# A transformer decoder on one core: four PSUM banks in one ring, query parts added on VectorE, two scalings on ScalarE, one tile for the rests of gates and values

## What is computed

```python
for i in range(DEPTH):                       # 6 layers
    x = attn_layer(shift_tokens(x), ...) + x # 16 heads of 64, window 64, rotary, l2norm of q and k
    x = ffn_layer(shift_tokens(x), ...) + x  # layernorm, 256 -> 2 x 682, a * gelu(gate), 682 -> 256
```

## Time and profile before

| | us |
|---|---|
| median of three runs | 2921.83 |
| the profiled execution | 2921.92 |
| its span, first to last instruction | 2920.1 |
| PE busy | 2776.2 (95%) |
| PE weight loads busy | 2447.4 (84%) |
| DVE busy | 2311.1 (79%) |
| ACT busy | 1978.6 (68%) |
| POOL (GpSimd) busy | 1362.4 (47%) |

### The profile page before, as it was taken

How to read it: one execution, slowest core, us unless ns; L and a number is a source line. 1 busy time by engine, 2 the same in 40 slices (tenths; PEclk the granted TensorE clock), 3 DMA queues, 4 the chain that set the end, 5 groups by cost and what they waited for, 6 DMA issues and landing times. The chain is left out here.

```text
span 2920.1 us, 80983 instructions
## 1 busy us (share of the span) xinstructions
PE 2776.2 (95%) x26408; PEld 2447.4 (84%) x26408; DVE 2311.1 (79%) x7881; ACT 1978.6 (68%) x5719; POOL 1362.4 (47%) x1436
## 2 busy tenths in 40 slices
PE   8889999999999999999999999999999999999996
PEld 6668888888888888888888888888888888888885
DVE  5478888878888888888877888887888877887773
ACT  4367767767776776777667667766776776676663
POOL 4454444535444453544445454544444453545440
PEclk9999999999999999999999999999999999999997
DMA  5212132333213324221333222143213233110110
GB/s 163 73 37 82 63 107 76 133 98 109 82 63 107 114 82 138 83 82 63 122 102 127 81 91 82 63 141 128 83 64 106 76 133 99 54 31 23 38 26 21
DMA packets 140063, 251.67 MB, mean 86 GB/s; under 512 B 14718, under 2 KB 78728, under 8 KB 138632
## 3 DMA queue, kind: packets, MB, share of 16 engines
q1 hardware_dynamic: 139224, 249.36, 26.0%
q10 hardware_dynamic: 688, 0.39, 0.0%
HBM read 137.72 MB, written 80.55 MB: 75 GB/s over the span
## 5 line engine op out<-in xcount | busy, mean ns | idle before, releaser
L904 PE MATMUL project<-w_qkv,xT 128*128 128x512 f32 x3456 | 892.0, 402 | 16.6 <-DVE with_sin L1275 11.8
L904 PEld LDWEIGHTS project<-w_qkv,xT 128*128 128x128 f32 x3456 | 621.9, 188 | 154.9 <-issue 12.4
L1179 POOL TENSOR_SCALAR sums_sq<-sums_sq 128x8 f32<-128x8 f32 x384 | 92.2, 240 | 1243.8 <-DVE sums_sq L1270 1238.3
L1124 ACT ACTIVATE probs<-probs,shift 128x128 f32<-128x128 f32 x1536 | 595.2, 390 | 73.6 <-DVE shift L1343 73.2
L1343 DVE CUSTOM_DVE_ANT_0 probs<-score,mask,query_scale 128x128 f32<-128x128 f32 x1536 | 439.8, 347 | 161.4 <-PE score L996 150.6
L959 PE MATMUL wide<-nT,w_up 128*128 128x256 f32 x3456 | 478.9, 288 | 13.8 <-ACT gates L1105 3.6
L959 PEld LDWEIGHTS wide<-nT,w_up 128*128 128x128 f32 x3456 | 439.8, 191 | 44.7 <-ACT gates L1105 24.0
L1355 DVE TENSOR_SCALAR probs<-probs,sums 128x128 f32<-128x128 f32 x1536 | 426.6, 341 | 13.6
L1073 ACT ACTIVATE with_sin<-project 128x512 f32<-128x512 f32 x384 | 230.5, 600 | 188.8 <-PE project L904 188.5
L1188 POOL TENSOR_TENSOR sums_sq<-sums_sq,half 128x8 f32<-128x8 f32 x192 | 321.4, 1674 | 16.0
L1185 POOL TENSOR_TENSOR query_scale<-sums_sq,half 128x8 f32<-128x8 f32 x192 | 317.7, 1655 | 22.2 <-POOL sums_sq L1179 12.3
(11 more groups left out here) (119 smaller groups left out, 4656.4 us busy)
## 6 DMA issues: line engine op xcount, KB each, us to landing
w_parts_scratch<-staging SPq DMA_DIRECT2D x120, 519.0 KB, 3.0
staging<-in_w_next SPq DMA_DIRECT2D x60, 519.0 KB, 5.0
w_qkv<-w_parts_scratch SPq DMA_DIRECT2D x20, 1536.0 KB, 9.2
v_mid<-v SPq DMA_DIRECT2D x192, 128.0 KB, 2.3
w_up<-w_parts_scratch SPq DMA_DIRECT2D x20, 682.0 KB, 6.3
y_in<-y_scratch SPq DMA_DIRECT2D x48, 256.0 KB, 3.7
res<-y_scratch SPq DMA_DIRECT2D x48, 256.0 KB, 2.7
y_scratch<-res SPq DMA_DIRECT2D x40, 256.0 KB, 4.1
```

The source lines that it names most:

```text
L904: last = pe.matmul(project[(x - 1) % 2][:], xT[a][:, h, t * P:(t + 1) * P], w_qkv[w][:, h, c, g, :], start=(h == 0 and (a, w) == PASSES[0] ...
L1124: last = act.activation(probs[:, k, cols], probs[:, k, cols], ACT.Exp, bias=shift[:, k, i:i + 1], scale=-1.0, accum_out=sums[:, k, i:i + 1])
```

## The change

- **Ring.** `project`, `turned` and `wide` give way to `ring`, four banks taken in turn by all fills of `input`, `unit`, `turn`, `turned`, `norm_turn`, `gate` and `value`, in `PE_ORDER`; the last one, `turned 3 1`, takes the bank two further on. `bank_free` now waits for the readers of the fill that had the same bank before (`fill_before`). Semaphores are counted by kind of fill.
- **Query parts.** DVE adds `with_sin` into `with_cos` for a query (128x512), and PE transposes four pieces as for a key.
- **Scalings.** Of the eight scalings of two heads in a slot, `scale 0 1` and `scale 3 0` are done by ACT (four `Copy` activations with a scale), after an `inverse` on DVE.
- **Rests.** The 42 columns of the values and, from row 64, the 42 of the gates share one 128-column tile, made with `gate 2`; `value 2` has one tile. A new DVE item `rest` multiplies them. A layer's fetch of `w_up` has four more DMAs (42 columns each).
- **Orders.** All four lists are changed, and the item `exp_table` (a tiny Exp that loads the table ahead of `exp 3 0`) is gone. Slot 1 is written out.

```diff
+RING = 4
...
 PE_ORDER = [
-    ("scores", 0), ("mix", 3), ("unit", 1, 0), ("unit", 1, 1), ("project_out", 0), ("unit", 1, 2), ("unit", 1, 3),
-    ("turned", 0, 0), ("project_out", 1), ("turned", 0, 1), ("turn", 1, 0), ("turn", 1, 1),
-    ("scores", 1), ("mix", 0), ("turn", 1, 2), ("unit", 1, 4), ("unit", 1, 5), ("turn", 1, 3), ("turned", 1, 0), ("norm_turn",),
-    ("input",), ("turned", 1, 1),
-    ("scores", 2), ("mix", 1), ("unit", 0, 0), ("unit", 0, 1), ("gate", 0), ("turned", 2, 0), ("unit", 0, 2), ("gate", 1),
-    ("unit", 0, 3), ("turned", 2, 1), ("gate", 2),
-    ("scores", 3), ("mix", 2), ("value", 0), ("turn", 0, 0), ("unit", 0, 4), ("value", 1), ("down", 0), ("turn", 0, 1),
-    ("turn", 0, 2), ("value", 2), ("down", 1), ("turned", 3, 0), ("unit", 0, 5), ("turn", 0, 3), ("turned", 3, 1), ("down", 2),
+    ("scores", 0), ("mix", 3), ("unit", 1, 0), ("unit", 1, 1), ("unit", 1, 2), ("project_out", 0), ("unit", 1, 3),
+    ("project_out", 1), ("turned", 0, 0), ("turned", 0, 1), ("turn", 1, 1),
+    ("scores", 1), ("mix", 0), ("unit", 1, 5), ("unit", 1, 4), ("turn", 1, 0), ("turn", 1, 3), ("turned", 1, 0), ("turn", 1, 2),
+    ("input",), ("turned", 1, 1), ("norm_turn",),
+    ("scores", 2), ("mix", 1), ("unit", 0, 0), ("gate", 0), ("gate", 1), ("unit", 0, 1), ("gate", 2), ("value", 0),
+    ("unit", 0, 2), ("turned", 2, 0), ("unit", 0, 3), ("turned", 2, 1),
+    ("scores", 3), ("mix", 2), ("value", 1), ("down", 0), ("unit", 0, 5), ("value", 2), ("turn", 0, 2), ("turn", 0, 1),
+    ("down", 1), ("unit", 0, 4), ("turn", 0, 3), ("turned", 3, 0), ("turn", 0, 0), ("down", 2), ("turned", 3, 1),
 ]
 ACT_ORDER = [
-    ("out", 3), ("unit", 1, 0), ("unit", 1, 1), ("exp", 0, 0), ("exp", 0, 1), ("unit", 1, 2), ("unit", 1, 3), ("copied", 0, 0),
-    ("copied", 0, 1), ("split_high", 0, 0), ("turn", 1, 0), ("turn", 1, 1), ("split_high", 0, 1), ("exp", 1, 0), ("turn", 1, 2),
-    ("out", 0), ("unit", 1, 4), ("exp", 1, 1), ("unit", 1, 5), ("turn", 1, 3), ("copied", 1, 0), ("input",), ("copied", 1, 1),
-    ("norm_turn",), ("exp", 2, 0), ("unit", 0, 0), ("exp", 2, 1), ("unit", 0, 1), ("gate", 0), ("copied", 2, 0), ("out", 1),
-    ("unit", 0, 2), ("gate", 1), ("unit", 0, 3), ("copied", 2, 1), ("gate", 2), ("exp_table",), ("exp", 3, 0), ("value", 0),
-    ("split_high", 1, 0), ("turn", 0, 0), ("split_high", 1, 1), ("unit", 0, 4), ("out", 2), ("value", 1), ("exp", 3, 1),
-    ("turn", 0, 1), ("turn", 0, 2), ("value", 2), ("copied", 3, 0), ("unit", 0, 5), ("turn", 0, 3), ("copied", 3, 1),
+    ("out", 3), ("unit", 1, 0), ("unit", 1, 1), ("exp", 0, 0), ("exp", 0, 1), ("unit", 1, 2), ("scale", 0, 1),
+    ("split_high", 0, 0), ("split_high", 0, 1), ("unit", 1, 3), ("copied", 0, 0), ("copied", 0, 1), ("turn", 1, 1),
+    ("exp", 1, 0), ("exp", 1, 1), ("unit", 1, 5), ("unit", 1, 4), ("turn", 1, 0), ("turn", 1, 3), ("copied", 1, 0),
+    ("turn", 1, 2), ("out", 0), ("input",), ("copied", 1, 1), ("norm_turn",), ("exp", 2, 0), ("unit", 0, 0), ("exp", 2, 1),
+    ("gate", 0), ("unit", 0, 1), ("gate", 1), ("out", 1), ("gate", 2), ("split_high", 1, 0), ("unit", 0, 2), ("copied", 2, 0),
+    ("value", 0), ("copied", 2, 1), ("unit", 0, 3), ("split_high", 1, 1), ("out", 2), ("exp", 3, 0), ("value", 1),
+    ("unit", 0, 5), ("exp", 3, 1), ("scale", 3, 0), ("turn", 0, 2), ("value", 2), ("turn", 0, 1), ("unit", 0, 4),
+    ("copied", 3, 0), ("turn", 0, 3), ("turn", 0, 0), ("copied", 3, 1),
 ]
 DVE_ORDER = [
-    ("mask", 0, 0), ("mask", 0, 1), ("out", 3), ("rotate", 1, 0), ("rotate", 1, 1), ("scale", 0, 0), ("scale", 0, 1),
-    ("rotate", 1, 2), ("rotate", 1, 3), ("add_out",), ("mask", 1, 0), ("norm_stats",), ("mask", 1, 1), ("scale", 1, 0),
-    ("norm_apply",), ("scale", 1, 1), ("split_low", 0, 0), ("out", 0), ("input",), ("mask", 2, 0), ("mask", 2, 1),
-    ("norm_turn",), ("scale", 2, 0), ("rotate", 0, 0), ("split_low", 0, 1), ("rotate", 0, 1), ("scale", 2, 1), ("out", 1),
-    ("rotate", 0, 2), ("rotate", 0, 3), ("mask", 3, 0), ("value", 0), ("low", 0), ("value", 1), ("mask", 3, 1), ("low", 1),
-    ("scale", 3, 0), ("value", 2), ("scale", 3, 1), ("low", 2), ("out", 2), ("split_low", 1, 0), ("split_low", 1, 1),
-    ("residual",),
+    ("mask", 0, 0), ("mask", 0, 1), ("out", 3), ("rotate", 1, 0), ("rotate", 1, 1), ("scale", 0, 0), ("inverse", 0, 1),
+    ("rotate", 1, 2), ("add_out",), ("rotate", 1, 3), ("mask", 1, 0), ("mask", 1, 1), ("norm_stats",), ("scale", 1, 0),
+    ("scale", 1, 1), ("norm_apply",), ("split_low", 0, 0), ("split_low", 0, 1), ("out", 0), ("input",), ("mask", 2, 0),
+    ("norm_turn",), ("mask", 2, 1), ("rotate", 0, 0), ("scale", 2, 0), ("scale", 2, 1), ("rotate", 0, 1), ("rest",),
+    ("value", 0), ("out", 1), ("rotate", 0, 2), ("mask", 3, 0), ("low", 0), ("rotate", 0, 3), ("value", 1), ("mask", 3, 1),
+    ("low", 1), ("inverse", 3, 0), ("out", 2), ("value", 2), ("low", 2), ("scale", 3, 1), ("residual",), ("split_low", 1, 0),
+    ("split_low", 1, 1),
 ]
 POOL_ORDER = [
-    ("rotate", 1, 0), ("rotate", 1, 1), ("rotate", 1, 2), ("rotate", 1, 3), ("norm_stats",), ("rotate", 0, 0), ("rotate", 0, 1),
-    ("norm_turn",), ("rotate", 0, 2), ("rotate", 0, 3),
+    ("rotate", 1, 0), ("rotate", 1, 1), ("rotate", 1, 2), ("rotate", 1, 3), ("norm_stats",), ("norm_turn",), ("rotate", 0, 0),
+    ("rotate", 0, 1), ("rotate", 0, 2), ("rotate", 0, 3),
 ]
 SHIFT_WIDE = 112
+ODD_FILL = ("turned", 3, 1)
...
+RING_FILLS, RING_BANK = [], []
+_next = 0
 for _item in PE_ORDER:
...
+    if _item[0] in ("unit", "turn", "turned", "input", "norm_turn", "gate", "value"):
+        for _half in range(HALVES if _item[0] == "input" else 1):
+            RING_FILLS.append((_item, _half))
+            if _item == ODD_FILL:
+                RING_BANK.append((_next + RING // 2) % RING)
+            else:
+                RING_BANK.append(_next)
+                _next = (_next + 1) % RING
+assert _next == 0
...
+def fill_before(n, item, half=0):
+    at, slots = RING_FILLS.index((item, half)), 0
+    j = at
+    while slots > -3:
+        j -= 1
+        if j < 0:
+            j, slots = j + len(RING_FILLS), slots - 1
+        if RING_BANK[j] == RING_BANK[at] and (not isinstance(n, int) or is_filled(n + slots, RING_FILLS[j][0])):
+            return n + slots, RING_FILLS[j]
+    return None
...
+    slot(Slot(1, next_batch=2, ffn_batch=0, chunk=0))
     for layer in range(DEPTH):
-        with eng.Fori(1, BATCH - 1) as b:
+        with eng.Fori(1 if layer else 2, BATCH - 1) as b:
...
-                dst = self.up[part][:, :, FFN:2 * FFN] if blk == 3 else self.up[part][:, :, 0:FFN]
+                at, rest = (FULL, 2 * FULL + GATE_REST) if blk == 3 else (0, 2 * FULL)
                 cols = cols.rearrange("p (k n) -> p k n", k=HALVES)
+                sp.dma_start(self.up[part][:, :, rest:rest + FFN_REST].bitcast(FP32), cols[:, :, FULL:FFN]).then_inc(self.fetched[blk], 16)
+                dst, cols = self.up[part][:, :, at:at + FULL], cols[:, :, 0:FULL]
...
-        project = [ctx.enter_context(nc.psum_tensor(f"project{i}", [P, GROUP], FP32)) for i in range(2)]
+        ring = [ctx.enter_context(nc.psum_tensor(f"ring{i}", [P, GROUP], FP32)) for i in range(RING)]
         score = [ctx.enter_context(nc.psum_tensor(f"score{i}", [P, GROUP], FP32)) for i in range(2)]
-        turned = ctx.enter_context(nc.psum_tensor("turned", [P, GROUP], FP32))
         mix = ctx.enter_context(nc.psum_tensor("mix", [P, 2, TOKENS], FP32))
...
-        wide = ctx.enter_context(nc.psum_tensor("wide", [P, 2, TOKENS], FP32))
...
+                if kind == "unit":
+                    g, u = item[1:]
+                    m = n if g else n + 1
+                    if u < 4:
+                        pe.wait_ge(parts_ready, rotation(m, g, u))
+                    else:
+                        pe.wait_ge(unit_read[g], unit_fill(m, g, u))
+                elif kind == "turn":
+                    g, u = item[1:]
+                    pe.wait_ge(turn_read[g], turn_fill(n if g else n + 1, g, u))
+                elif kind == "input":
+                    pe.wait_ge(input_read, (n + 1) * HALVES + half + 1)
+                    pe.wait_ge(input_split, (n + 1) * HALVES + half + 1)
+                elif kind == "turned":
+                    k, j = item[1:]
+                    pe.wait_ge(probsT_copied, n * HEADS + QUAD_HEADS * k + 2 * j + 2)
+                elif kind == "norm_turn":
+                    pe.wait_ge(xn_read, f + 1)
+                elif kind == "gate" and item[1] == 2:
+                    pe.wait_ge(rest_read, f + 1)
+                elif kind == "gate":
+                    pe.wait_ge(gate_read, f * 3 + item[1] + 1)
+                else:
+                    pe.wait_ge(value_read, f * 3 + item[1] + 1)
...
+                    if u % 2:
+                        pe.wait_ge(rotated, rotation(m, g, u))
+                    else:
+                        pe.wait_ge(query_added, m * 4 + 2 * g + u // 2 + 1)
+                    bank_free(s, item)
```

(50 more changed lines are left out.)

233 lines of the change are left out of this document (111 added, 122 removed).

## The result

The changed kernel takes **2720.1 us** (median of 4 runs, 2718.1 to 2723.1) against 2921.5 in the same session: ratio 0.931, 95% interval 0.930 to 0.933. The direction and most of the mechanism held. What was off is the stall, the time in a slot in which PE waits: it was taken at 3.0 us a slot and measures 2.2.

The account below looks back on a forecast made before the run. PE was taken to fill the slot of 56.70 us, with about 4.0 of it stall. Span 2920.1 - 118 (PE's work) - 46 (stall) + 9 (later transfer) = 2765, with 1.8 around the span 2767 us; range 2722 to 2800, chance 0.61.

Parts of the forecast that it names:

- the stall: PE's waiting time in a slot: forecast to fall from 4.0 to 3.0 us, 46 us over 46 slots.
- the later transfer: Raw chunks asked for later, behind y's later store: ACT waits some 1.3 us in 30 slots; +9 us, bounds 0 and 39.
- The walk: Following each wait through the four new lists with measured pitches: a slot of 52.7 us, stall 2.5.
- a stall of 1.7 behind ACT's copies: Between scores 1 and scores 2, the ring hands PE each bank only after ACT's copy: 1.7 of 9.6 us.
- the margin for hand-overs: Added to the walk's stall of 2.5 for small hand-over times and late transfers, giving 3.0 and a slot of 53.2.
- The stall of before: About 4.0 us of the old slot, largest before scores 2, where PE was said to wait for DVE's scaling and norm.
- PE's work: Fewer transposes (1.74 us a slot) and value matmuls (0.71): 2.45 us a slot, 118 us in 48 slots, all on the path.
- DVE: Four adds +2.44 us, eight scaling instructions -1.58, rest 0: net +0.9 a slot, to 48.4.
- ACT: Eight activations 128x128 come in at 0.30 us each: +2.4 us, ACT at 43.1 a slot.
- Work only: Rival: the ring's new waits cost what the old ones did, so only PE's work is saved; 2813 us, chance 0.18.
- DVE keeping its idle: Rival "slower": in-order lists leave DVE's 9.1 us of idle, slot 57.5 us, time 2959 us; chance 0.05.
- The GpSimd rival: Every query add on DVE waits 0.9 us for GpSimd's power: 2890 us; clearest mechanism of "part lost", chance 0.08.

Follow-up runs that it names:

- l: The kernel before with one edit: scale 0 1 moved from DVE to ACT, behind unit 1 2; 2859 us, ratio 0.980.
- e: The changed kernel with a query's two parts added by PE again (eight transposes a turn) and DVE's four adds gone; 2754 us, ratio 0.943.
- f: The changed kernel with value 2 given two tiles again, six more matmuls 128x256; 2745 us, ratio 0.940.
- p: The changed kernel with the lists of before, except rest ahead of mask 3 0 and scale 0 1 on ACT; ring kept; 2915 us, ratio 0.999.
- j: The changed kernel with only scale 0 1 put back on DVE, scale 3 0 staying on ACT; 2766 us, ratio 0.947.
- m: The changed kernel with split_low 1 before residual, split_high 0 after unit 1 3's square, Exp table fetched ahead, add_out after rotate 1 3, norm_stats after scale 1 0; 2735 us.
- g: The changed kernel with split_low 1 0 and 1 1 ahead of residual in DVE's list; 2719 us, ratio 0.931.
- h: The changed kernel with split_high 0 0 and 0 1 behind the square of unit 1 3 in ACT's list; 2717 us, ratio 0.930.
- c: The changed kernel with its new lists but the banks of before in place of the ring; 3333 us, ratio 1.142.

## Why the prediction was right or wrong

**The term that was mis-sized: the stall.** The sum let the stall fall from 4.0 to 3.0 us a slot, 46 us in all. Measured, the slot of 52.36 less the work of 50.2 leaves 2.2. So the slot is 0.84 us shorter than the 53.2 forecast, and that is 39 of the 47 us. The ends of the program (slot 47 to 48 in 48.4 instead of 53.9, the tail in 45.1 instead of 48.8) gave some 4 more than their work, and the rise above the plain pitch grew by 7 us (14 to 21) where the sum had 9 for the later transfer.

**Where the 0.8 a slot comes from.** The walk gave 14.8, 9.6 and 28.3; the timeline has 14.9, 8.8 and 28.6. It said 52.7, and 0.3 of the 0.8 is its error. Its sum is nearer than its parts: the stretch before scores 2, where it had a stall of 1.7 behind ACT's copies, has only 0.9 of it, and the other two are 0.1 and 0.3 longer than walked. The wait is of the kind forecast, and half the size; at which step the walk lost the difference isn't on record and stays open. The other 0.5 is the margin for hand-overs that I put on top, of which the steady slot shows nothing.

**The stall of before: a wrong reason.** I laid the waits before scores 2 to the place of DVE's norm and scalings in its list. l moves one scaling and leaves the norm where it was, and the slot falls by 1.1 us: over a quarter of the 4.0 hung on scale 0 1, which stood locked out behind GpSimd. The 4.0 is soft besides: what a like group takes at its shortest depends on what follows it (four transposes take 0.35 ahead of a unit and 0.43 or more ahead of other transposes), and 0.4 of it is the pace of the slot's last `down`, not a wait.

**PE's work: counts right, value half right.** 3168 and 1536 instructions, 2.45 us a slot. But "all of it is on the path" failed. Put back one at a time, the transposes are worth 34 of 84 us (e) and the tile 25 of 34 (f). PE was not the bound between scores 1 and scores 2. How the whole gain divides between less work and less stall the runs can't say, since each depends on the other: p has all of the work savings and is no faster than before.

**DVE: wrong sign, outside the sum.** I had +0.9 us a slot; measured is -0.7 (46.84 against 47.58). The adds came as priced: beside GpSimd's power they take 0.69, and 49 of 192 that meet its 128x512 operation take about 1.04 (timeline of DVE of the changed kernel):

```profile
1206.67 0.69 DVE L1350 TENSOR_TENSOR with_cos<-with_cos,with_sin 128x512 f32<-128x512 f32 x1
...
1212.04 1.04 DVE L1350 TENSOR_TENSOR with_cos<-with_cos,with_sin 128x512 f32<-128x512 f32 x1
```

What failed is the removal: I priced both scalings from one plain row of 0.88, when one of the two took 2.7 in every slot. The group's mean of 341 ns, where a plain one lasts 283, should have made me look. That one scaling is worth 46 us in the changed kernel (j) and 59 in the old (l). DVE's total was no term of the sum, and the walk had scale 0 1 on ACT already, so this mistake is in the account of the old stall and in the rivals' DVE times, not in the 52.7.

**ACT: near.** 42.51 a slot where 43.1 was forecast; a scaling takes 1.28 for four instructions. The table's load stands after the wait, and m, which fetches it ahead, is no proof either way.

**The later transfer: mechanism right, the short waits free, the long ones unpriced.** y's store stands 2.1 us after scores 0, as forecast, and ACT waits 28 times for the raw chunk. g and h show that PE doesn't see the short waits. The four of about 4 us at changes of layer were not foreseen; whether the 7 us of rise are theirs stays open.

**The rivals.** "Work only" at 2813 came out in no run with the old lists: the same parts give 3128 or, at best of those run, 2915. That also means that the risk of a slower kernel lay elsewhere than I put it. It was not DVE keeping its idle, but a bank held by `rest` or by a late rotation. The GpSimd rival (each add waiting for the power) is refuted: 136 adds inside a power took 0.69 to 0.71. The rule on the shared port, from "SBUF — State Buffer" of the Trainium skill, agrees with the trace where GpSimd's operation is 512 columns wide, and its line on `tensor_scalar`, in the section "Who interferes with whom", would have pointed at the 2.7 us, had I looked for what the change takes away and not only for what it adds.

## What to carry to other kernels

Price what a change removes as carefully as what it adds, with the longest and shortest duration of the group, not with one plain row; an instruction that is locked out shows no wait, only a longer duration. Work taken from the busiest engine counts only in the stretches where that engine is the bound: in the others it turns into waiting. Where each engine works down a fixed list, a new holder of a buffer and the lists must be changed together, and a walk through the lists with measured pitches came within 1% of the slot here, though one of its three stretches was 0.8 us off; a margin on top of it wants a reason of its own.

## What the runs showed of the hardware

- Four `TENSOR_SCALAR` 128x128 from SBUF to SBUF take 0.88 us on VectorE, and 2.5 to 2.8 while GpSimd runs its two 128x512 operations of 1.3 and 1.1 us. Beside GpSimd's power on 128x8 (1.66 us) they take 0.88.
- A 128x512 add on VectorE with both inputs in SBUF takes 0.69 beside that power and 0.84 to 1.5 beside a 128x512 operation of GpSimd: it ends about 0.55 after GpSimd does. A `TENSOR_TENSOR` of the same size with one input in PSUM (L1444 of the changed kernel) takes 0.65 to 0.68 also inside such an operation, 93 times of 93.
- The last `down` of a slot, whose second half has 42 rows, takes 1.75 to 1.80 us for its 12 matmuls in every kernel here, where the others take 1.37 or little more. I had counted those 0.4 us as stall.
- TensorE's granted clock was 0.95 to 0.97 in the steady slots of c and 1.00 in those of before and of the changed kernel. In c it was 0.63 in the 4.6 us right behind a wait of 2.96 us: part of them ran at the lower of its two levels, 1.2 GHz and not 2.4.
